# An embedding and interaction kernel: the last tile of 128 samples in four units of 32 samples, with the top layer of 96 of them summed apart

## What is computed

```python
emb = emb_tables[jnp.arange(NUM_FIELDS)[:, None], x_cat]
emb = jnp.transpose(emb, (1, 0, 2))
dense_embed = price[:, None] @ Wp + bp
feats = jnp.concatenate([emb, dense_embed[:, None, :]], axis=1)
gram = jnp.einsum('bid,bjd->bij', feats, feats)
interactions = gram[:, _IU, _JU]
h = jax.nn.relu(dense_embed @ W1 + b1)
dense_out = jax.nn.relu(h @ W2 + b2)
concat = jnp.concatenate([interactions, dense_out], axis=1)
t = jax.nn.relu(concat @ Wt1 + bt1)
out = (t @ Wt2 + bt2)[:, 0]
```

## Time and profile before

| what | value |
|---|---|
| three runs | 540.46, 543.34, 543.46 us (median 543.34) |
| the profiled execution | 542.15 us, its span 540.3 us |
| PE busy | 246.3 us, 46% |
| PE weight loads busy | 177.9 us, 33% |
| DVE busy | 145.4 us, 27% |
| ACT busy | 169.1 us, 31% |
| POOL busy | 393.8 us, 73% |
| mean granted TensorE clock | 0.70 |

### The profile page before, as it was taken

One profiled execution on the slowest core, in us unless ns is written; L12 is line 12 of the kernel. 1 busy time (PEld: TensorE's weight loads), 2 busy tenths in 40 slices (PEclk: granted clock), 3 DMA queues, 4 the chain that ended last, 5 costly groups with the idle time before them and its releaser, 6 DMA issues.

```text
span 540.3 us, 4362 instructions
## 1 busy us (share of the span) xinstructions
PE 246.3 (46%) x1496; PEld 177.9 (33%) x1496; DVE 145.4 (27%) x358; ACT 169.1 (31%) x405; POOL 393.8 (73%) x425
## 2 busy tenths in 40 slices
PE   0118033240569515134249733315136960565775
PEld 0105033240534304133234423305134440544654
DVE  3003233040331504123040331503233051333353
ACT  0124323041241604223042440503224052243563
POOL 6777777777777777777777777777777777777750
PEclk9999665555659856555577975755555985669798
DMA  6233333333323333333333333333332333332210
GB/s 187 26 26 27 26 28 27 26 27 27 26 27 27 26 27 28 26 26 27 26 29 26 27 27 26 27 27 27 26 27 26 26 28 26 26 28 27 28 22 2
DMA packets 14360, 16.26 MB, mean 30 GB/s; under 512 B 7169, under 2 KB 7425, under 8 KB 14209
## 3 DMA queue, kind: packets, MB, share of 16 engines
q0 software_dynamic: 13312, 13.66, 30.9%
q1 hardware_dynamic: 578, 2.19, 1.1%
q10 hardware_dynamic: 448, 0.14, 0.1%
HBM read 15.95 MB, written 0.01 MB: 30 GB/s over the span
## 4 chain that ended last, share of the span: by engine, by line
POOL 68%; issue 26%; DMA 2%; PE 2%; ACT 1%; DVE 0%; POOLq 0%
POOL gathered L200 68%; DMA gathered<-in_table,row_idx 2%; PE ps_mlp L487 1%; ACT gram L141 1%; PE ps_trans L419 1%; DMA raw_idx<-in_x_cat 0%; POOLq L50 0%; PE ps_gram L456 0%; PE ps_mlp L479 0%; PE ps_mlp L495 0%; DVE feats L166 0%; DVE top L368 0%; ACT scores L279 0%; DVE row_idx L339 0%; DVE wrapped L332 0%
## 5 line engine op out<-in xcount | busy, mean ns | idle before, releaser
L200 POOL DMA_INDIRECT gathered<-in_table,row_idx x416 | 392.7, 944 | 128.0 <-issue 125.9
L419 PE MATMUL ps_trans<-ident,gathered 128*128 128x128 f32 x208 | 45.4, 381 | 223.0 <-DMA gathered<-in_table,row_idx 223.0
L456 PE MATMUL ps_gram<-feats 64*128 64x128 f32 x1024 | 105.2, 384 | 61.0 <-ACT gram L141 30.2
L141 ACT COPY gram<-ps_gram 32x112 f32<-32x112 f32 (+1 forms) x272 | 97.2, 357 | 108.1 <-PE ps_gram L456 105.2
L141 DVE COPY gram<-ps_gram 32x112 f32<-32x112 f32 (+1 forms) x272 | 96.6, 355 | 116.8 <-PE ps_gram L456 113.5
L456 PEld LDWEIGHTS ps_gram<-feats 64*128 64x128 f32 x1024 | 96.9, 286 | 75.4 <-issue 52.6
L419 PEld LDWEIGHTS ps_trans<-ident,gathered 128*128 128x128 f32 x208 | 35.0, 198 | 236.3 <-issue 234.9
L151 ACT COPY feats<-ps_trans 64x448 f32<-64x448 f32 (+1 forms) x60 | 34.1, 569 | 195.4 <-PE ps_trans L419 195.0
L151 DVE COPY feats<-ps_trans 64x448 f32<-64x448 f32 (+1 forms) x60 | 36.8, 613 | 203.3 <-PE ps_trans L419 202.7
L487 PE MATMUL ps_mlp<-gram,wt1p_sb 128*128 128x512 f32 (+2 forms) x168 | 60.2, 520 | 2.9 <-ACT gram L141 2.9
L487 PEld LDWEIGHTS ps_mlp<-gram,wt1p_sb 128*128 128x128 f32 x168 | 32.6, 228 | 32.6 <-issue 28.0
(11 more groups left out here) (24 smaller groups left out, 33.5 us busy)
## 6 DMA issues: line engine op xcount, KB each, us to landing
gathered<-in_table,row_idx POOLq DMA_INDIRECT x416, 3.3
price_bc<-in_price SPq DMA_DIRECT2D x1, 1024.0 KB, 5.2
wt1p_sb<-in_wt_pairs SPq DMA_DIRECT2D x1, 896.0 KB, 7.8
raw_idx<-in_x_cat SPq DMA_DIRECT2D x1, 195.0 KB, 2.7
w_sb<-in_w ACTq DMA_DIRECT2D x2, 32.0 KB, 4.8
wt1d_sb<-in_wt_dense ACTq DMA_DIRECT2D x1, 64.0 KB, 7.7
raw_idx<-in_x_cat SPq DMA_DIRECT2D x1, 13.0 KB, 1.8
consts_sb<-in_consts ACTq DMA_DIRECT2D x1, 4.5 KB, 2.0
```

What stands on the lines that cost most here:

```text
L141: last = copy(gram_to[QUAD * c:QUAD * (c + 1), n % 2, t - BATCHES[n][0], :, rg * r:rg * (r + 1), :, s], source[QUAD * s:QUAD * (s + 1), :, ...
L200: pool.indirect_dma_start(out=gathered[:, to * D:(to + 1) * D], out_offset=None, in_=rows, in_offset=bass.IndirectOffsetOnAxis(ap=row_idx[ ...
L419: last = nc.tensor.transpose(ps_trans[:, to + k * P:to + (k + 1) * P], gathered[:, base + f * D:base + (f + 2) * D], ident[:, :])
L456: last = nc.tensor.matmul(ps_gram[:, out_at:out_at + P], group, group, start=True, stop=True)
```

## The change

The last tile is cut into four units of 32 samples, 16 of each half. A gather now fetches four fields of 32 samples each. Six gathers hold 24 of the 26 fields of one unit; a seventh with units 0 and 2 holds the two fields left over, for two units. So units are gathered by 7, 6, 7 and 6 DMAs, and each has its own transposes, its own copies to `feats` (VectorE has two more in units 0 and 2, line 174 of the changed kernel, for the shared gather), and its own round of products. The top layer of the last tile is cut as well: `top_part(m, 0, 3)` sums 96 samples of the first three units in `ps_mlp` once round 2 is copied, `top_part(m, 1, 4)` sums the last 32 in `ps_trans`. Each part has its own relu. The base per field of the last tile is no longer made by two IOTAs but added from `field_base` in twelve small additions. `WARM` is now 2, 6, 6, 1: before the transposes of units 1, 2 and 3, and before the products of unit 3.

The diff, without declarations, removed helpers and the host's index layout:

```diff
-UNITS = 2
-UNIT = HALF // UNITS
+UNITS = 4
+UNIT = P // UNITS
+SIDE = UNIT // 2
+COLS = FIELDS // UNITS
+SHARED = UNITS * COLS
...
-LAST_CHUNKS = [(0, 8), (8, 16), (16, 24), (24, 26)]
-LAST_ROUNDS = 4
+PAIR = 2 * COLS + 1
+UNIT_COLS = [[PAIR * (n // 2) + (COLS + 1) * (n % 2) + g for g in range(COLS + 1 - n % 2)] for n in range(UNITS)]
+EARLY = (UNITS - 1) * SIDE
+LAST_ROUNDS = UNITS
 LAST_RG = GROUPS // LAST_ROUNDS
 
...
-WARM = (0, 7, 3, 1, 1)
-TO_GRAM, TO_TOP = 4, 5
+WARM = (2, 6, 6, 1)
+TO_GRAM = 4
...
+        def evacuate_unit(copy, n, kk):
+
+            src = ps_trans[D * kk:D * (kk + 1), BANK * (n % 2):BANK * (n % 2) + COLS // 2 * P]
+            src = src.rearrange("p (m q h b) -> p h m q b", m=COLS // 2, q=UNITS, h=2)
+            for h in range(2):
+                dst = feats[D * h:D * (h + 1), SIDE * n:SIDE * (n + 1), 1:1 + SHARED]
+                dst = dst.rearrange("p b (m k q) -> p k m q b", m=COLS // 2, k=2, q=UNITS)
+                last = copy(dst[:, kk], src[:, h])
             return last
+
+        def evacuate_shared(copy, n):
+
+            at = BANK * (n % 2) + COLS // 2 * P
+            src = ps_trans[0:D, at:at + P].rearrange("p (w e h b) -> p h w e b", w=2, e=2, h=2)
+            for h in range(2):
+                dst = feats[D * h:D * (h + 1), SIDE * n:SIDE * (n + 2), SLOTS - 2:SLOTS]
+                last = copy(dst.rearrange("p (w b) e -> p w e b", w=2), src[:, h])
+            return last
...
+        def last_gram(j):
+            at = ((last_batch % 2) * SLABS + j) * WIDE * P
+            return halves(gram[:, at:at + P])
+
+        def last_part(m, late):
+
+            if not late:
+                return slice(0, EARLY), halves(ps_mlp[m][:, 0:P])[:, :, 0:EARLY]
+            return slice(EARLY, HALF), halves(ps_trans[:, BANK * m:BANK * m + UNIT])
...
+            pool.wait_ge(rows_made, 2 + 3 * UNITS)
             pool.wait_ge(chunk_transposed[0], LAST)
-            for c, (f0, f1) in enumerate(LAST_CHUNKS):
-                if c == 1:
+            for n in range(UNITS):
+                if n == 2:
                     pool.wait_ge(chunk_transposed[1], LAST)
-                for f in range(f0, f1):
-                    gather(LAST, f, last_gathered[c])
+                for col in UNIT_COLS[n]:
+                    gather(LAST, col, unit_gathered[n])
...
             dense_out_relu(n)
-            for r in range(LAST_ROUNDS // 2):
-                gram_round(r, t)
-            odd_last(2)
-            odd_last(3)
-            for r in range(LAST_ROUNDS // 2, LAST_ROUNDS):
-                gram_round(r, t)
-            top_relu(n)
+            gram_round(0, t)
+            gram_round(1, t)
+            odd_unit(2)
+            gram_round(2, t)
+            odd_unit(3)
+            part_relu(0)
+            gram_round(3, t)
+            part_relu(1)
...
-            nc.vector.tensor_tensor(row_idx[:, b:e], clamped[:, b:e], last_base[:, :], ALU.add)\
-                .then_inc(rows_made, 1)
+            for q in range(UNITS):
+                part = slice(UNIT * q, UNIT * (q + 1))
+                to = row_idx[part, b:e].rearrange("p (k c) -> p k c", c=PAIR)
+                from_ = clamped[part, b:e].rearrange("p (k c) -> p k c", c=PAIR)
+                base = field_base[part, 0:SHARED].rearrange("p (o g q) -> p q o g", o=1, q=UNITS)[:, q]
+                for c in (0, COLS + 1):
+                    nc.vector.tensor_tensor(to[:, :, c:c + COLS], from_[:, :, c:c + COLS],
+                                            base.to_broadcast([UNIT, 2, COLS]), ALU.add).then_inc(rows_made, 1)
+                nc.vector.tensor_tensor(to[:, :, COLS], from_[:, :, COLS],
+                                        field_base[part, SHARED + q % 2:SHARED + q % 2 + 1].to_broadcast([UNIT, 2]),
+                                        ALU.add).then_inc(rows_made, 1)
...
+            def even_unit(n):
+                dve.wait_ge(unit_transposed, n + 1)
+                if n % 2 == 0:
+                    evacuate_shared(nc.vector.tensor_copy, n)
+                evacuate_unit(nc.vector.tensor_copy, n, 0).then_inc(trans_evac_dve, 1)
...
+            even_unit(1)
+            gram_round(0, t)
+            gram_round(1, t)
+            even_unit(2)
+            gram_round(2, t)
+            even_unit(3)
+            gram_round(3, t)
+            part_relu(0)
+            part_relu(1)
...
+            def transpose_unit(n):
+
+                wait_trans_evac(NC * LAST + max(n - 1, 0))
+                keep_warm(n, n % 2)
+                pe.wait_ge(unit_gathered[n], 16 * len(UNIT_COLS[n]))
+                base = (LAST % BUFFERS) * ROW
+                for m in range(COLS // 2):
+                    at, to = base + UNIT_COLS[n][2 * m] * D, BANK * (n % 2) + m * P
+                    last = nc.tensor.transpose(ps_trans[:, to:to + P], gathered[:, at:at + 2 * D], ident[:, :])
+                if n % 2 == 0:
+                    at, to = base + UNIT_COLS[n][COLS] * D, BANK * (n % 2) + COLS // 2 * P
+                    last = nc.tensor.transpose(ps_trans[0:D, to:to + P], gathered[:, at:at + D], ident[:, :])
+                last.then_inc(unit_transposed, 1)
...
             def gram_last(r):
-                if r == LAST_ROUNDS // 2:
-
-                    wait_trans_evac(NC * LAST + len(LAST_CHUNKS) - 1)
+                wait_trans_evac(NC * LAST + r + 1)
+                if r == LAST_ROUNDS - 1:
                     keep_warm(TO_GRAM, 0)
-                wait_trans_evac(NC * LAST + (2 if r < LAST_ROUNDS // 2 else len(LAST_CHUNKS)))
                 pe.wait_ge(dense_slot_set, 2 * TILES)
                 wait_gram_evac(ROUNDS * LAST + max(r - 1, 0))
                 gram_matmuls(LAST_RG * r, LAST_RG, 2 * BANK * (r % 2), BANK).then_inc(gram_done, 1)
...
-                        if BATCHES[n][1] == TILES:
-                            keep_warm(TO_TOP, 1)
-                        wait_gram_evac(ROUNDS * BATCHES[n][1] + (LAST_ROUNDS - ROUNDS if BATCHES[n][1] == TILES else 0))
+                        wait_gram_evac(ROUNDS * BATCHES[n][1])
...
+            def top_part(m, late, rounds):
+
+                part, to = last_part(m, late)
+                pe.wait_ge(dense_out_made, last_batch + 1)
+                nc.tensor.matmul(to, wt1d_sb[:, m * P:(m + 1) * P], halves(dense_out[:, 0:P])[:, :, part],
+                                 start=True, stop=False)
+                wait_gram_evac(ROUNDS * LAST + rounds)
+                for j in range(SLABS):
+                    last = nc.tensor.matmul(to, wt1p_sb[:, j * TM1 + m * P:j * TM1 + (m + 1) * P], last_gram(j)[:, :, part],
+                                            start=False, stop=(j == SLABS - 1))
+                last.then_inc(top_summed[m], 1)
+
             def score(n):
 
-                pe.wait_ge(top_made, 2 * n + 2)
+                pe.wait_ge(top_made, 2 * n + (4 if n == last_batch else 2))
...
-            transpose_last(0)
+            transpose_unit(0)
             top_layer(n - 1)
-            transpose_last(1)
+            transpose_unit(1)
             score(n - 1)
             hidden_layer(n)
             dense_out_layer(n)
-            for r in range(LAST_ROUNDS // 2):
-                gram_last(r)
-            transpose_last(2)
-            transpose_last(3)
-            for r in range(LAST_ROUNDS // 2, LAST_ROUNDS):
-                gram_last(r)
-            top_layer(n)
+            gram_last(0)
+            gram_last(1)
+            transpose_unit(2)
+            gram_last(2)
+            top_part(0, 0, 3)
+            transpose_unit(3)
+            gram_last(3)
+            top_part(1, 0, 3)
+            for m in range(2):
+                top_part(m, 1, UNITS)
             score(n)
```

76 lines of the change are left out of this document (30 added, 46 removed).

## The result

| | before | after |
|---|---|---|
| median | 542.81 us (540.46 to 543.93, 6 runs) | 551.66 us (549.67 to 554.24, 6 runs) |
| ratio after / before | | 1.0164, 95% interval 1.0129 to 1.0200 |
| profiled execution, span | 542.15, 540.3 us | 551.76, 550.0 us |
| PE, DVE, ACT busy | 246.3, 145.4, 169.1 us | 253.2, 147.1, 168.8 us |
| mean granted TensorE clock | 0.70 | 0.70 |

The change makes the kernel slower by 8.9 us, 1.64%. The forecast was 6.1 us, and 548.5. The measured 551.66 lies just above the range, which ended at 551.6.

A forecast was written before the change was run, and what follows sets the result against it. GpSimd's gathers were taken to bound the kernel (68% of the span), with the change acting on the tail behind them. Full-clock chain +4.4 and half-clock stretch +1.7 gave +6.1 on the 542.4 mean: 548.5 us, range 545.2 to 551.6.

The forecast's parts named there:

- clock term: One stretch at half TensorE clock after the lull, from early top layer to unit 3's transposes: +1.7 us.
- steps 4 to 6: Early top layer for m=0, six keep-warm matmuls, unit 3's transposes and copies to `feats`: 527.7 to 533.7 at full clock.
- step 0: VectorE's copies of rounds 0 and 1: net +0.25 us from the change's work there, ending at 522.7.
- B: Rival: short streams are cheap, so the late top layer's 32-column records shrink; +3.3 us, 545.7; 10%.
- E: Rival: each top-layer record costs its weight load and its stream one after the other; +8.0 us, 550.4; 3%.
- steps 4 and 5: Early top layer for m=0, 1.6 us, then six keep-warm matmuls ahead of unit 3's transposes, 2.6 us, at full clock.
- steps 9 and 10: Late top layer of the last 32 samples, 3.9 us, then relu, score, store and DMA, 3.22 us, ending at 544.7.
- Case C: Rival: half clock from early top layer through unit 3's transposes, nothing regained; +8.9 us, 551.3; 11%.
- step 6: Unit 3's three transposes, 0.6 us, and their copies, 2 x 0.484 and 0.1 us, ending at 533.7.
- +4.4: Sum of the rebuilt tail's chain at full clock, in us: end at 544.7 against 540.3 before.
- D: Rival: unit 3 starts when its rows land, at 524.78, and the end comes earlier; -2.8 us, 539.6; 4%.

The follow-up runs named there:

- e2: Changed kernel with unit 3's transposes and their keep-warm matmuls moved ahead of the early top layer for m=0: 547.24 us, ratio 1.0112.
- e3: Changed kernel with the last tile's top layer in one piece again, behind all four rounds: 548.10 us, ratio 1.0093.
- e20: Changed kernel with whole top layer at the end, dense layers behind products, keep-warm matmuls ahead of unit 3's transposes replaced by five behind: 541.62 us, ratio 0.9984.
- e17: The changed kernel itself run once more, as control on another chip: 551.83 us, ratio 1.0175 to the kernel before.
- e10: Changed kernel with six more keep-warm matmuls on each side of unit 2's products: 549.36 us, ratio 1.0138.
- e12: Kernel before with only the last tile's top layer cut into 96 and 32 samples as in the changed kernel: 543.60 us, ratio 1.0025.
- e18: Changed kernel with the last batch's dense layers behind the products of rounds 0 and 1 instead of ahead: 548.86 us, ratio 1.0118.
- e19: Kernel before with the last batch's dense layers behind the products of rounds 0 and 1 instead of ahead: 541.92 us, ratio 0.9994.
- e21: e20 with one keep-warm matmul behind unit 3's transposes instead of five: 662.21 us, ratio 1.0093, on a chip where before takes 654.89.
- e1: Changed kernel without the six keep-warm matmuls ahead of unit 3's transposes: 551.60 us, ratio 1.0147.
- e22: e21 with six more keep-warm matmuls between unit 2's transposes and products: 661.48 us, ratio 1.0069, on a chip where before takes 654.89.

## Why the prediction was right or wrong

Step by step, the duration of each from the rows above against the forecast's:

| step | forecast | measured | difference |
|---|---|---|---|
| 0, copies of rounds 0 and 1 end | at 522.7 | at 524.4 | +1.7 |
| 1 to 3, unit 2 to `feats`, products, copies | 5.0 | 4.95 | 0 |
| 4, early top part, m=0 | 1.7 | 3.2 | +1.5 |
| 5, six keep-warm matmuls | 2.6 | 3.65 | +1.05 |
| 6 to 8, unit 3, its products and copies | 5.6 | 5.65 | 0 |
| 9, late top parts | 3.9 | 4.55 | +0.65 |
| 10, relu, score, store | 3.2 | 3.55 | +0.35 |
| clock term, for steps 4 to 6 | 1.7 | in steps 4 to 10 | -1.7 |
| end of the span | 546.4 | 550.0 | +3.6 |

Two terms of the sum were too small: the clock term, 1.7 us forecast and 3.55 measured, and step 0, +0.25 forecast and +2.0 measured. The rest came out.

- **Mechanism: right.** The chain ran as the steps say: unit 3 stood behind unit 2's products, the early part's wait and the keep-warm matmuls. Its transposes began without a DMA in front, unit 2's six keep-warm matmuls were hidden behind the copies, and the early part for m=1 was hidden with 0.3 us to spare (539.75 + 1.80 = 541.55, copies until 541.86), where the forecast had 0.6. e2 and e3 show the order's share, 3 to 4 us, and e20, in which unit 3 waits for the DMA again, has its chain through the last gather. Gathers, IOTAs and the 12 additions cost nothing.
- **Records bound by their weights: right.** 0.112 us for 32 columns; B falls (14 records in 1.72 us, where a quarter of 0.112 each would give 0.4), and so does E, load and stream in a row (it would need 0.137 a record).
- **The clock term: too small.** "I expect one stretch at half clock, under steps 4 to 6, at no less than the 1.65": that is the first step that failed. The half clock lasted 6.83 us (527.83 to 534.66), twice before's 3.35, and cost 2.55 us in steps 4 and 5; it came back from 544.90 on and cost 1.0 in steps 9 and 10. That is 3.55 against 1.7 in all. e17 shows the same pattern, and e10, in which the clock is full from 513.5 to 544.2, has steps 4 and 5 2.5 us shorter. Case C, half clock under all of steps 4 to 6, was priced at 551.3 and given 11%; what came is nearest to it in time, but not as C has it: the clock was back before step 6, and C's price came together only with the stretch at the end and the late entry, so that it lies near is luck.
- **Step 0: too small.** "Net +0.25" priced what the change does there and took for granted that the tail is entered when before's was. It was entered 1.85 us later (TensorE at the earlier batch's top layer at 509.00, before at 507.15), all of it half clock in tile 14. Before absorbs about 1 us of such a delay, because it waits for the landing (e12); the changed chain has no wait left to absorb it. e18 and e19 show both sides. The forecast should have said that the +4.4 has a spread of some 2 us on one side, and the range should have gone up to 553.
- **D, faster:** its landing-bound start was not to be had in this order. e20 shows that start in another order, and that it still gives only 0.2%, since a fill in the wrong place and a top layer of full length follow.
- The traces differ by 9.7 us and the medians by 8.9, since the traced execution of before, 542.15, was 0.66 below its median and that of the changed kernel, 551.76, was 0.10 above.

What stays open: why the clock falls in tile 14 in one trace and not in another, whether the change has a part in it, what makes the gathers of five traces 1.0 us late, and whether e21 beats e20 where before takes 542 us.

## What to carry over

A finer last unit helps only if each engine's program lets it start when its data land: look for what stands in front of it in program order, and for waits in front of that. Count small matmuls by the columns of their weights; four times fewer streamed columns saved nothing here, and cutting a layer in two doubled its time. Keep-warm matmuls paid in the waits on both sides of unit 2's products (e10), though they did not hold the clock in every trace; on the chain, or behind the fall of the clock, they are the next thing that everyone waits for. A kernel whose end hangs on a DMA's landing forgives delays upstream up to the length of its wait, and a change that takes this anchor away pays for all of them. Look which gather the chain that ended last goes through: it says at once whether an end is anchored.

## What the runs showed of the hardware

Twelve keep-warm records take 2.78 to 2.86 us at the full clock, and ten take 4.39 at half (e20), so they are dearest where they are wanted most. Without keep-warm matmuls ahead of unit 3 the clock did not come back at all for 24 us (e1: 0.50 from 526.8 to the end, though TensorE was busy for 15.16 of the 17.00 us up to 551.0); with six of them it came back after 6.8.

There are two kinds of chip here: on two of them before takes 655 and 660 us with the same program. The gathers are as fast there, but GpSimd stands idle between them for longer. This is the page's group of e21:

```profile
L216 POOL DMA_INDIRECT gathered<-in_table,row_idx x416 | 392.6, 944 | 219.2 <-issue 121.0
```

219.2 us idle against 128.0 in the earlier trace rows, at the same 944 ns a gather. Single waits of TensorE reach 12.3 us (e22) and 17.6 us (e21) in tile 14, and more than half of the chain that ended last (57% in e21) is put down to another core or a queue that the profile does not know. What holds the engines there stays open.
